# A 3x3 convolution by four products for two neighbouring columns, in a four-layer kernel on one Trainium2 core

## The chip, the cores and the metric

The kernel runs on one core of one Trainium2 chip. The metric is the device time of the whole program in microseconds (us). Before the change it is 9030.84 us, the median of three runs from 9029.97 to 9038.97 us. The engines are TensorE (PE, its weight loads PEld), VectorE (DVE), ScalarE (ACT), GpSimd (POOL) and SyncE (SP).

## What is computed

Four layers in a row on x of shape (16, 192, 32, 32), all in f32. The change touches layer 0 alone. Per image, `seq` is the image as 1024 positions of 192 channels:

```python
x1 = _vil_block(seq, ln_w, ln_b, w_up, ...)       # norm, up, causal filter, gated scan, norm, gate, down, + seq
x2 = silu(seq @ w_lin + b_lin)
y = x1 + x2                                       # (16, 192, 32, 32)
y = conv_general_dilated(y, conv2_w, (1, 1), ((1, 1), (1, 1)))     # 192 to 192 channels, 3 x 3
y = y + conv2_b
y = (y - mean) / sqrt(var + 1e-05) * bn_g + bn_b  # mean, var over images and positions
return where(y >= 0, y, 0.01 * y)
```

The kernel stores the convolution's result with its bias in the DRAM tensor `y`, with statistics for mean and variance; what follows is done when layer 1 reads it.

## The kernel before, in words

All engines run their own list of instructions; the order in each list is written out by hand in `stages`, and semaphores (`S.mark`, `wait_ge(*S(...))`) tie the lists together. Each part of the work is a generator with the same number of `yield` steps on every engine, so that a step stands at the same place in every list. For image b of layer 0:

- five steps of `conv(b - 1)`;
- eight steps of `project(b)`: ACT makes `xa` (line 844) from the filter that DVE ran in the join (lines 738 and 742); PE the gates (911) and then q and k (934), DVE and ACT the gates' arithmetic (794 to 886);
- two more steps of `conv(b - 1)`, and then the rest of `project`: PE's decay products (942, 948), DVE's `gam` (830) and `qt` (836);
- the scan, 24 steps (`chunks`), woven with the other 11 of `conv(b - 1)`; from its ninth step on also with `ahead(b + 1)`, the norms of the next image (lines 472 to 527 and 680 to 765). PE makes scores (1052), the outputs (1017, 1022), the state (1031) and transposes (1040, 1045); DVE spreads q (1086), multiplies (1099, 1105) and updates the state (1072, 1078); ACT takes exponentials (1131) and copies the outputs (1119); POOL adds the mask (966) to rows that SP fetches (979, 991);
- the norm of the scan's outputs (DVE 1150 to 1176, ACT 1186 to 1194), woven with `enter(b + 1)`, PE's up products (705, 708);
- the join: `lin` (1212 to 1218), transposes (1226), gates of the next image (898), `down` (1239, 1237), DVE's skip and gate (1255, 1257), and y in three parts (1264): y 0 is channels 0 to 127 of image rows 0 to 15, y 1 channels 128 to 191 of both halves of the rows (one half on partitions 0 to 63, the other on 64 to 127), y 2 channels 0 to 127 of rows 16 to 31.

The convolution reads the padded images `ypa` (34 x 34) and `ypb` (18 x 34 for each half; ACT copies the row of the other half, lines 1278 and 1279, 64x32). It has 18 steps, all f32. In the first nine, one for each tap, PE makes outputs 0 to 127 in two banks, one for each half of the rows: two products 128 to 128 on 512 columns (1298) and two 64 to 128 on the upper and the lower rows of the array (1300). In the other nine it makes outputs 128 to 191 of both halves in one bank: two products 128 to 64 (1312) and two 64 to 64 (1314). ACT evacuates with the bias to `yo` (1326), DVE takes bn_stats (1334), SP stores (1340, 1344).

PSUM is eight banks of 512 f32 columns, handed out in turn (`Banks.take`; `hold` keeps a bank out of the turn until `drop`): who is given a bank waits until the last user's data were read.

## Time and profile before

| | before |
|---|---|
| median of the runs | 9030.84 us |
| profiled execution, time | 9027.38 us |
| profiled execution, span | 9025.6 us, mean granted PE clock 0.899 |
| PE busy | 7558.3 us, 84% of the span |
| DVE busy | 5897.5 us, 65% |
| ACT busy | 3432.4 us, 38% |
| POOL busy | 1928.0 us, 21% |

Layer 0 takes the first fifteen of the profile's forty slices. One image's pass of its loop is some 206 us. In the profile a line number is that of the kernel; one f32 product of PE stands as two records.
### The profile page before, as it was taken

How to read it: one execution, taken by the hardware profiler on the slowest of the kernel's cores; microseconds unless marked ns; L12 is line 12 of the kernel's file. 1: busy time of each engine (PE TensorE's matmuls, PEld its weight loads, DVE VectorE, ACT ScalarE, POOL GpSimd, SP SyncE). 2: the span in 40 equal slices, each digit the busy share in tenths (PEclk: the TensorE clock that was granted, in tenths of full speed). 3: DMA queues.
4: the chain of work that ended last, by engine and by line, in shares of the span. 5: the costliest groups of instructions: out<-in, count | busy, mean ns of one | idle time of the engine just before them, and what ended most of it. 6: DMA issues, size and time to landing. Idle time of an engine off the chain costs nothing.

```text
span 9025.6 us, 92796 instructions
## 1 busy us (share of the span) xinstructions
PE 7558.3 (84%) x34478; PEld 3447.9 (38%) x34478; DVE 5897.5 (65%) x10339; ACT 3432.4 (38%) x6408; POOL 1928.0 (21%) x1639
## 2 busy tenths in 40 slices
PE   7999999999999994678888888888888888888855
PEld 4444444444444441133333333333333333333333
DVE  4666666666666654267766766776776776676645
ACT  3443343433434322443343254253344334334410
POOL 1111111111111110031331232142143133123223
PEclk8999999999999995779988989888898998888987
DMA  1111111111111111034544445454455454454446
GB/s 63 36 36 36 36 41 37 44 45 42 39 37 36 36 34 66 14 130 123 143 154 123 130 153 145 109 163 142 109 163 153 120 151 154 112 138 154 135 125 171
DMA packets 251362, 874.73 MB, mean 97 GB/s; under 512 B 47436, under 2 KB 50200, under 8 KB 250528
## 3 DMA queue, kind: packets, MB, share of 16 engines
q1 hardware_dynamic: 157440, 413.88, 17.1%
q0 software_dynamic: 92160, 453.06, 15.8%
q8 instruction: 274, 4.49, 0.2%
q10 hardware_dynamic: 1312, 1.87, 0.1%
q14 instruction: 176, 1.44, 0.1%
HBM read 614.69 MB, written 102.26 MB: 79 GB/s over the span
## 4 chain that ended last, share of the span: by engine, by line
PE 62%; DVE 18%; ACT 8%; DMA 4%; issue 3%; SPq 3%; POOL 0%; ACTq 0%; DVEq 0%; POOLq 0%
PE ps L2115 9%; PE ps L2348 6%; PE ps L2551 4%; PE ps L1052 4%; PE ps L1298 3%; DVE arena L1825 3%; PE ps L1022 3%; PE ps L2125 3%; SPq L2585 3%; PE ps L934 3%; PE ps L2562 3%; PE ps L2053 2%; DMA arena<-arena 2%; PE ps L2039 2%; PE ps L1300 2%
## 5 line engine op out<-in xcount | busy, mean ns | idle before, releaser
L2381 POOL DMA_INDIRECT arena<-img,arena x1152 | 1368.1, 1188 | 2845.4 <-DMA img<-arena 1988.8
L966 POOL TENSOR_TENSOR arena<-arena 128x512 f32<-128x512 f32 x384 | 438.0, 1146 | 2773.3 <-DMA arena<-decay 2773.3
L2242 DVE SCALAR_TENSOR_TENSOR arena<-arena 128x384 f32<-128x384 f32 x1152 | 745.7, 647 | 431.1 <-DMA arena<-img,arena 426.9
L1825 DVE TENSOR_REDUCE arena<-ps 128x2 f32<-128x1024 f32 x768 | 896.2, 1218 | 192.6 <-PE ps L2094 187.3
L1969 ACT ACTIVATE arena<-ps 128x512 f32<-128x512 f32 x1536 | 816.9, 603 | 395.7 <-PE ps L2125 394.5
L2551 PE MATMUL ps<-arena 128*64 128x512 f32 x3072 | 803.0, 651 | 137.0 <-DMA arena<-arena 136.9
L2115 PE MATMUL ps<-arena 128*64 128x512 f32 x3072 | 911.0, 697 | 0.0
L2348 PE MATMUL ps<-arena 128*96 128x128 f32 x4608 | 649.3, 304 | 110.5 <-DVE arena L2231 110.5
L2348 PEld LDWEIGHTS ps<-arena 128*96 128x96 f32 x4608 | 605.9, 186 | 265.4 <-issue 265.4
L2125 PE MATMUL ps<-arena 32*128 32x512 bf16 x1536 | 352.3, 433 | 227.2 <-ACT arena L1976 128.1
L1052 PE MATMUL ps<-arena 128*128 128x512 f32 x768 | 452.0, 673 | 81.8 <-DVE arena L1072 47.4
L934 PE MATMUL ps<-arena 128*128 128x512 f32 x1152 | 507.2, 596 | 0.0
L1099 DVE TENSOR_TENSOR arena<-ps,arena 128x512 f32<-128x512 f32 x384 | 265.7, 692 | 327.6 <-PE ps L1052 291.0
L2248 DVE SCALAR_TENSOR_TENSOR arena<-arena 128x192 f32<-128x192 f32 x1152 | 477.3, 415 | 0.0
L1131 ACT ACTIVATE arena<-arena 128x128 f32<-128x128 f32 x1536 | 476.4, 389 | 0.4
L2551 PEld LDWEIGHTS ps<-arena 128*64 128x64 f32 x3072 | 213.8, 145 | 542.8 <-issue 542.5
L1086 DVE COPY arena<-arena 32x128 f32<-32x128 f32 x1536 | 402.3, 262 | 16.8
L2094 PE MATMUL ps<-arena 32*128 32x512 bf16 x1536 | 293.7, 425 | 119.2 <-DVE arena L1825 93.8
L1022 PEld LDWEIGHTS ps<-arena 128*128 128x128 f32 x3072 | 390.5, 199 | 0.0
L1022 PE MATMUL ps<-arena 128*128 128x33 f32 x3072 | 390.5, 273 | 0.0
L2513 ACT ACTIVATE arena<-ps 128x512 f32<-128x512 f32 x128 | 76.7, 600 | 819.7 <-PE ps L2551 819.7
L2125 PEld LDWEIGHTS ps<-arena 32*128 32x128 bf16 x1536 | 75.7, 93 | 787.0 <-ACT arena L1969 577.0
(334 smaller groups left out, 11585.1 us busy)
## 6 DMA issues: line engine op xcount, KB each, us to landing
arena<-arena SPq DMA_DIRECT2D x1024, 144.5 KB, 2.8
arena<-decay SPq DMA_DIRECT2D x384, 256.0 KB, 3.3
img<-arena SPq DMA_DIRECT2D x162, 384.0 KB, 2.4
arena<-y SPq DMA_DIRECT2D x32, 768.0 KB, 5.7
arena<-img,arena POOLq DMA_INDIRECT x1152, 4.6
arena<-x SPq DMA_DIRECT2D x32, 384.0 KB, 6.5
y<-arena SPq DMA_DIRECT2D x32, 384.0 KB, 3.2
out<-arena SPq DMA_DIRECT2D x16, 768.0 KB
```

Source lines behind the costliest of these rows:

```text
L934: i = pe.matmul(ps[:, :], w[:, c, 128 * m:128 * m + 128], xa[:, c, H(h)], start=c == 0, stop=c == 2)
L1022: i = pe.matmul(po[:, 33 * h:33 * h + 33], px[:, 128 * j:128 * j + 128], v1[:, 33 * h:33 * h + 33], start=False, stop=j == 3)
L1052: pe.matmul(ps[:, :], kk[:, g, sl], self.qd[n % 3].rearrange("p a b -> p (a b)"), start=True, stop=True).then_inc(*S.mark("s_pe", b, n))
L1825: dve.tensor_reduce(out, self.wides[B.at("max", b, g, n, h) // 2].rearrange("p (a b) -> p a b", a=2), AX.X, AL.max).then_inc(*S.mark("max_ ...
L1969: act.activation(self.p[n % 6], B("score", b, n)[:, :], ACT.Exp).then_inc(*S.mark("p_act", b, n))
L2115: pe.matmul(o[64 * m:64 * m + 64, :], self.va[:, tb, 64 * hd:64 * hd + 64], self.p[n % 6], start=tb == 0, stop=tb == 7).then_inc(*S.mark(" ...
L2125: pe.matmul(ps[:, :], ks[r, hd // 3, 128 * tb:128 * tb + 128], qs[r, hd // 3, H(h)], start=True, stop=True).then_inc(*S.mark("score_pe", b ...
L2242: dve.scalar_tensor_tensor(gb[:, 0:384], gb[:, 384:768], pp[:, 1, n:n + 1], gb[:, 0:384], AL.mult, AL.add).then_inc(*S.mark("corner_x", b, n))
L2248: dve.scalar_tensor_tensor(self.tk[n // 9 % 2][:, n % 9, :], gb[:, 192:384], pp[:, 0, n:n + 1], gb[:, 0:192], AL.mult, AL.add).then_inc(*S ...
L2348: i = pe.matmul(ps[0:96, 128 * k:128 * k + 128], tk[:, tap, 96 * k:96 * k + 96], C["ID"], start=tap == 0, stop=tap == 8)
L2381: pool.indirect_dma_start(self.g[n % 6], None, img, bass.IndirectOffsetOnAxis(ap=ii[:, n:n + 1], axis=0)).then_inc(*S.landed(f"gather{n % ...
L2551: i = pe.matmul(ps[64 * t:64 * t + 64, :], self.dg[J % 2][:, o:o + 2, :].rearrange("p a b -> p (a b)"), win, start=n == 0, stop=n == 2)
```

## The change

For two neighbouring columns 2n and 2n + 1 of the output and each row y of the filter g, four products take the place of six. With d0 to d3 the four input columns 2n to 2n + 3 of the padded image, the input parts are d0 - d2, d1 + d2, d2 - d1 and d3 - d1, the filter parts g0, (g0 + g1 + g2)/2, (g0 - g1 + g2)/2 and g2. The product of part 1 and the one of part 2 with their sum and difference, and parts 0 and 3 on top of these, give the two columns.

- Filter parts: DVE makes them once in the setup, eight instructions on 576 elements, behind `prep0`. Part 1 takes the place of g1, part 2 is `u2`.
- Images: `ya` (34 x 34) and `yb`, now 50 x 34: rows 0 to 33 of it on partitions 64 to 127 and 16 to 49 on 0 to 63 are the whole padded image. ACT therefore copies 16 rows each way (64x512). Both lie where the scan's outputs `osb` and the gates `gb` lie, and POOL clears them in each norm.
- Input parts: POOL makes them in the join from every second column. "upper" (four instructions, 17 x 16) after y 0, "last" (four of 64 partitions, 34 x 16) after both halo copies, "lower" (four, 17 x 16) after y 2. `va` lies over `zs`, whose next writer waits for the convolution's end.
- Products: 18 steps in three thirds (outputs 0 to 127 of either half of the rows, outputs 128 to 191), each in two banks, two steps for each row of the filter. All have 256 columns. A step of the first two thirds is two products 128 to 128 and two 64 to 128; one of the last third four 128 to 64 and four 64 to 64, one for each quarter of the array.
- Evacuation: ACT takes one product with the bias (256 columns), DVE adds 512 columns, then 256 twice, then bn_stats, for each third; the y stores wait for DVE. Each stands at steps 7, 13 and 19 instead of 10 (two at once) and 19.

POOL no longer clears `ypa` and `ypb` in the setup, and the arena in SBUF grows by 700 columns. The diff, without context lines and without these two:

```diff
@@ -556,9 +556,13 @@
+        yr = Arena(ar.tile, ar.at)
-        self.ypa = ar([128, 34, 34])
-        self.ypb = ar([128, 18, 34])
+        self.ya, self.yb = yr([128, 34, 34]), yr([128, 50, 34])
+        self.va = [z.rearrange("p a b -> p (a b)")[:, 0:2176].rearrange("p (q r n) -> p q r n", q=4, r=34) for z in self.zs]
+        self.vb = ar([128, 2, 34, 16])
+        self.u2 = ar([128, 2, 3, 192])
+        self.p1 = ar([128, 256])
@@ -636,6 +640,16 @@
+        for k in range(2):
+            u = self.u2[:, k]
+            g = [W["C2"][:, k, :].rearrange("p (y x n) -> p y x n", y=3, x=3)[:, :, x, :] for x in range(3)]
+            dve.tensor_tensor(u, g[0], g[2], AL.add).then_inc(*S.mark("prep0", "u", k, 0))
+            dve.wait_ge(*S("prep0", "u", k, 0))
+            dve.tensor_tensor(u, u, g[1], AL.subtract).then_inc(*S.mark("prep0", "u", k, 1))
+            dve.wait_ge(*S("prep0", "u", k, 1))
+            dve.scalar_tensor_tensor(g[1], u, 0.5, g[1], AL.mult, AL.add).then_inc(*S.mark("prep0", "u", k, 2))
+            dve.wait_ge(*S("prep0", "u", k, 2))
+            dve.tensor_scalar(u, u, 0.5, None, AL.mult).then_inc(*S.mark("prep0", "u", k, 3))
@@ -768,6 +782,7 @@
+        act.wait_ge(*S("conv_pe", b - 2, 2))
@@ -848,6 +863,7 @@
+        act.wait_ge(*S("parts", b - 1, "lower"))
@@ -1255,17 +1271,15 @@
-        for n, inner in enumerate((self.ypa[:, 1:17, 1:33], self.ypb[:, 1:17, 1:33], self.ypa[:, 17:33, 1:33])):
+        for n, inner in enumerate((self.ya[:, 1:17, 1:33], self.yb[:, 17:33, 1:33], self.ya[:, 17:33, 1:33])):
-            dve.wait_ge(*S("conv_pe", b - 1, 2))
-            if n == 1:
-                dve.wait_ge(*S("halo", b - 1, 1))
+            dve.wait_ge(*S("zero", "pad", b))
@@ -1275,71 +1289,107 @@
-        act.activation(ypb[0:64, 17, 1:33], ypb[64:128, 1, 1:33], ACT.Copy).then_inc(*S.mark("halo", b, 0))
-        act.activation(ypb[64:128, 0, 1:33], ypb[0:64, 16, 1:33], ACT.Copy).then_inc(*S.mark("halo", b, 1))
+        act.activation(yb[0:64, 33:49, 1:33], yb[64:128, 17:33, 1:33], ACT.Copy).then_inc(*S.mark("halo", b, 0))
+        act.activation(yb[64:128, 1:17, 1:33], yb[0:64, 17:33, 1:33], ACT.Copy).then_inc(*S.mark("halo", b, 1))
+    def pool_norm(self, pool, b):
+        yield from skip(7)
+        pool.wait_ge(*self.S("norm_dve", b, "inv"))
+        pool.memset(self.ya, 0.0)
+        pool.memset(self.yb, 0.0).then_inc(*self.S.mark("zero", "pad", b))
+        yield
+    def pool_join(self, pool, b):
+        S, ya, yb, va, vb = self.S, self.ya, self.yb, self.va[b % 2], self.vb
+        parts = ((0, 2, AL.subtract), (1, 2, AL.add), (2, 1, AL.subtract), (3, 1, AL.subtract))
+        pool.wait_ge(*S("zero", "pad", b))
+        for key, r0, r1 in (("upper", 0, 17), ("last", 0, 34), ("lower", 17, 34)):
+            if key == "last":
+                pool.wait_ge(*S("conv_pe", b - 1, 2))
+                pool.wait_ge(*S("halo", b, 1))
+                for n, q in enumerate((0, 3, 1, 2)):
+                    h, (i, j, op) = n // 2, parts[q]
+                    if n == 2:
+                        pool.wait_ge(*S("parts", b, "upper"))
+                    r, y = slice(64 * h, 64 * h + 64), yb[64 * h:64 * h + 64, 16 - 16 * h:50 - 16 * h, :]
+                    t = pool.tensor_tensor(vb[r, n % 2], y[:, :, i:i + 31:2], y[:, :, j:j + 31:2], op)
+            else:
+                pool.wait_ge(*S("join_dve", b, "y", 0 if key == "upper" else 2))
+                if key == "lower":
+                    pool.wait_ge(*S("parts", b, "last"))
+                for q, (i, j, op) in enumerate(parts):
+                    t = pool.tensor_tensor(va[:, q, r0:r1, :], ya[:, r0:r1, i:i + 31:2], ya[:, r0:r1, j:j + 31:2], op)
+            t.then_inc(*S.mark("parts", b, key))
+    def filter_part(self, k, y, q, m):
+        return self.u2[:, k, y, m] if q == 2 else self.W["C2"][:, k, 576 * y + 192 * (q, q, 0, 2)[q]:576 * y + 192 * (q, q, 0, 2)[q] + 192][:, m]
-        S, B, W = self.S, self.B, self.W["C2"]
+        S, B, va, vb, part = self.S, self.B, self.va[b % 2], self.vb, self.filter_part
-        out = []
-        for h in range(2):
-            ps, free = B.hold(("conv", b, h), ("conv_act", b, h))
-            pe.wait_ge(*free)
-            out.append(ps)
-        pe.wait_ge(*S("join_dve", b, "y", 2))
-        pe.wait_ge(*S("halo", b, 1))
-        for tap in range(9):
-            y, x = divmod(tap, 3)
-            w = slice(192 * tap, 192 * tap + 128)
-            for h in range(2):
-                pe.matmul(out[h][:, :], W[:, 0, w], self.ypa[:, 16 * h + y:16 * h + y + 16, x:x + 32], start=tap == 0, stop=False)
-            for h, r in enumerate(both):
-                i = pe.matmul(out[h][:, :], W[r, 1, w], self.ypb[r, y:y + 16, x:x + 32], start=False, stop=tap == 8)
-                if tap == 8:
-                    i.then_inc(*S.mark("conv_pe", b, h))
-            yield
-        for h in range(2):
-            B.drop(("conv", b, h))
-        ps, free = B.hold(("conv", b, 2), ("conv_act", b, 2))
-        pe.wait_ge(*free)
-        for tap in range(9):
-            y, x = divmod(tap, 3)
-            w = slice(192 * tap + 128, 192 * tap + 192)
-            for h, r in enumerate(both):
-                pe.matmul(ps[r, :], W[:, 0, w], self.ypa[:, 16 * h + y:16 * h + y + 16, x:x + 32], start=tap == 0, stop=False)
-            for h, r in enumerate(both):
-                i = pe.matmul(ps[r, :], W[r, 1, w], self.ypb[r, y:y + 16, x:x + 32], start=False, stop=tap == 8)
-            if tap == 8:
-                i.then_inc(*S.mark("conv_pe", b, 2))
-            yield
-        B.drop(("conv", b, 2))
+        flat = lambda v: v.rearrange("p r n -> p (r n)")
+        pe.wait_ge(*S("prep0", "u", 1, 3))
+        pe.wait_ge(*S("parts", b, "lower"))
+        for n in range(3):
+            banks = []
+            for q, by in enumerate(("first", "y")):
+                ps, free = B.hold(("conv", b, n, q), ("conv_dve", b, n, by))
+                pe.wait_ge(*free)
+                banks.append(ps)
+            out = [banks[q in (1, 2)][:, 256 * (q in (2, 3)):256 * (q in (2, 3)) + 256] for q in range(4)]
+            m = slice(128, 192) if n == 2 else slice(0, 128)
+            halves = list(enumerate(both)) if n == 2 else [(n, slice(0, 128))]
+            for y in range(3):
+                for n2, pair in enumerate(((0, 1), (3, 2))):
+                    rows = lambda h: slice(16 * h + y, 16 * h + y + 16)
+                    for q in pair:
+                        for h, r in halves:
+                            pe.matmul(out[q][r, :], part(0, y, q, m), flat(va[:, q, rows(h), :]), start=y == 0 and n2 == 0, stop=False)
+                    for t, q in zip(both, pair):
+                        for h, r in halves:
+                            i = pe.matmul(out[q][r, :], part(1, y, q, m)[t], flat(vb[t, n2, rows(h), :]), start=False, stop=y == 2 and n2 == 1)
+                    if y == 2 and n2:
+                        i.then_inc(*S.mark("conv_pe", b, n))
+                    yield
+            for q in range(2):
+                B.drop(("conv", b, n, q))
+        S = self.S
+        for n in range(3):
+            yield from skip(6)
+            act.wait_ge(*S("conv_pe", b, n))
+            act.wait_ge(*S("conv_dve", b if n else b - 1, n - 1 if n else 2))
+            act.activation(self.p1, self.B("conv", b, n, 1)[:, 0:256], ACT.Identity, bias=self.W["C2B"][:, n // 2:n // 2 + 1]).then_inc(*S.mark("conv_act", b, n))
+    def dve_conv(self, dve, b):
-            if n != 1:
-                yield from skip(9)
-            act.wait_ge(*S("conv_pe", b, n))
-            act.activation(self.yo[:, n, :], B("conv", b, n)[:, :], ACT.Identity, bias=self.W["C2B"][:, n // 2:n // 2 + 1]).then_inc(*S.mark("conv_act", b, n))
-    def dve_conv(self, dve, b):
-        S = self.S
-        for n in range(3):
-            if n != 1:
-                yield from skip(9)
+            yield from skip(6)
+            one, two = B("conv", b, n, 0), B("conv", b, n, 1)
+            y = self.yo[:, n, :].rearrange("p (n s) -> p s n", s=2)
+            dve.tensor_tensor(y, one.rearrange("p (s n) -> p s n", s=2), self.p1.unsqueeze(1).to_broadcast([128, 2, 256]), AL.add).then_inc(*S.mark("conv_dve", b, n, "first"))
+            dve.wait_ge(*S("conv_dve", b, n, "first"))
+            dve.tensor_tensor(y[:, 0, :], y[:, 0, :], two[:, 256:512], AL.add)
+            dve.tensor_tensor(y[:, 1, :], y[:, 1, :], two[:, 256:512], AL.subtract).then_inc(*S.mark("conv_dve", b, n, "y"))
+            dve.wait_ge(*S("conv_dve", b, n, "y"))
-        yield from skip(9)
-        sp.wait_ge(*S("conv_act", b, 1))
+        yield from skip(12)
+        sp.wait_ge(*S("conv_dve", b, 1, "y"))
-        yield from skip(9)
-        sp.wait_ge(*S("conv_act", b, 2))
+        yield from skip(6)
+        sp.wait_ge(*S("conv_dve", b, 2, "y"))
@@ -1389,7 +1439,7 @@
-                    lambda b: skip(8), lambda b: None, lambda b: skip(18))
+                    lambda b: self.pool_norm(e, b), lambda b: self.pool_join(e, b), lambda b: skip(18))
...
```

## Rows read from the trace of the kernel before

**Rows 1.** the page, second part: TensorE's busy tenths in forty slices of the span

```profile
PE   7999999999999994678888888888888888888855
```

**Rows 2.** timeline of PE, join to gates: start us, us, engine line operation

```profile
669.06 2.85 PE L1226 MATMUL ps<-arena 128*128 128x128 f32 x24 [1.15 <-DVE arena L1176]
...
686.08 1.98 PE L1298 MATMUL ps<-arena 128*128 128x512 f32 x4 [1.14 <-DVE arena L1264]
687.99 1.13 PE L1300 MATMUL ps<-arena 64*128 64x512 f32 x4
689.05 1.99 PE L1298 MATMUL ps<-arena 128*128 128x512 f32 x4
...
700.95 2.79 PE L911 MATMUL ps<-arena 128*64 128x512 f32 x12
```

**Rows 3.** timeline of PE, products of 256 columns: layer 3, then layer 2

```profile
7040.02 7.17 PE L2532 MATMUL ps<-arena 96*128 96x256 f32 x32 [0.31 <-DVE arena L2441]
...
4234.32 7.99 PE L2307 MATMUL ps<-arena 96*32 96x256 f32 x144 [1.25 <-ACT arena L2274]
```

**Rows 4.** timeline of PE, products to the next norm

```profile
737.11 1.88 PE L1298 MATMUL ps<-arena 128*128 128x512 f32 x4
...
742.96 0.24 PE L942 MATMUL ps<-arena 76*128 76x8 bf16 x3
...
748.54 2.04 PE L1052 MATMUL ps<-arena 128*128 128x512 f32 x2 [1.93 <-DVE arena L1086]
...
767.90 1.08 PE L1312 MATMUL ps<-arena 128*64 128x512 f32 x4
...
769.92 1.13 PE L1052 MATMUL ps<-arena 128*128 128x512 f32 x2
...
838.60 1.81 PE L1052 MATMUL ps<-arena 128*128 128x512 f32 x2 [3.34 <-DVE arena L1072]
...
875.12 2.85 PE L1226 MATMUL ps<-arena 128*128 128x128 f32 x24 [1.15 <-DVE arena L1176]
```

**Rows 5.** timeline of VectorE, join, y 1 and y 2

```profile
682.22 0.69 DVE L1264 TENSOR_TENSOR arena<-ps,arena 128x512 f32<-128x512 f32 x1 [0.25 <-PE ps L1237]
...
685.34 0.69 DVE L1264 TENSOR_TENSOR arena<-ps,arena 128x512 f32<-128x512 f32 x1
```

**Rows 6.** ScalarE: durations min/median/max of line 755, then two rows of its timeline

```profile
L755 ACT ACTIVATE arena<-arena x32: 621/626/630, 62.2 to 3090.3; 64x512 f32<-64x512 f32 x32
...
690.74 1.06 ACT L844 ACTIVATE arena<-arena 128x1024 f32<-128x1024 f32 x1 [4.22 <-DVE arena L742]
...
737.93 1.05 ACT L886 ACTIVATE arena<-arena 12x1024 bf16<-12x1024 f32 x1
```

**Rows 7.** GpSimd by line, durations ns min/median/max

```profile
L966 POOL TENSOR_TENSOR arena<-arena x384: 1087/1093/2077, 121.1 to 3294.7; 128x512 f32<-128x512 f32 x192
...
L2571 POOL TENSOR_TENSOR arena<-arena x64: 1498/1508/1527, 4075.8 to 8976.7; 128x768 f32<-128x768 f32 x64
```

**Rows 8.** VectorE by line, durations ns min/median/max, with and without GpSimd at work

```profile
L824 DVE TENSOR_TENSOR arena<-arena x16: 1521/1903/2141, 122.5 to 3200.7; 12x1024 f32<-12x1024 f32 x16
...
L827 DVE TENSOR_TENSOR arena<-arena x16: 1211/1214/1216, 129.6 to 3207.8; 12x1024 f32<-12x1024 f32 x16
```

**Rows 9.** windows (PE clock last but two), then timeline of PE

```profile
842.00:844.00 2.00, 2.00 (x6) 0.56 (x6) 0.41 (x2) 1.56 (x5) 0.00 (x0) 0.50 0.00 0
3328.00:3330.00 2.00, 2.00 (x10) 1.70 (x8) 1.97 (x4) 0.00 (x0) 0.00 (x0) 0.50 0.00 0
...
3324.72 5.38 PE L1226 MATMUL ps<-arena 128*128 128x128 f32 x24 [14.54 <-DVE arena L1176]
```

**Rows 10.** timeline of VectorE, opening of the scan, and behind the scan

```profile
743.54 3.68 DVE L836 TENSOR_TENSOR arena<-arena,ps 128x512 f32<-128x512 f32 x6
...
852.37 0.69 DVE L1334 BATCH_NORM_STATS2 arena<-arena 128x6 f32<-128x512 f32 x1 [2.57 <-ACT arena L1326]
```

**Rows 11.** waits of VectorE from 669.06 to 875.12: us in total, times, longest

```profile
DVE arena L1099 <- PE ps L1052: 20.5, 12, 4.7
```

12 lines of the change are left out of this document (6 added, 6 removed).

## The prediction

> **What bounds the kernel now.** I read first the page's slices: in the first fifteen of the forty, which are layer 0, TensorE's (PE's) digit is 9 but for the first [rows 1]. Then the order of time on PE in one batch of layer 0, from the transposes at 669.06 us to the same transposes of the next batch at 875.12 us [rows 2, 4]: 206.1 us a batch. In it PE's starts follow each other with hardly a gap. So layer 0 is bound by PE's program order, but closely followed by VectorE (DVE): where PE does wait, DVE releases it, before line 1052 at 748.54 us (1.93 us) and at 838.60 us (3.34 us) and before 1226 (1.15 us) [rows 4]. The convolution of batch b lies in four places: five steps right after the join, two after the q and k products, eleven woven into the scan of batch b+1; for the last batch all eighteen in a row. What a step saves is worth what that place allows, so I work place by place and take the batch from 669 to 875 us as the model of fifteen.
>
> **The product itself.** An old step with 128 outputs is 1.91 us for the two full products and 1.06 us for the pair on half the rows, 2.97 together (starts at 686.08, 687.99 and 689.05) [rows 2]. An old step of the last 64 outputs is 2.02 us, from 767.90 to 769.92 [rows 4]. One f32 product stands as two records. 256 columns cost 0.22 us a record (32 in 7.17 us), and with four column tiles at work 0.055 us (144 in 7.99 us) [rows 3]. So of the old step 4 x 0.44 + 2 x 0.44 = 2.64 us is streaming and 0.33 us is what the two switches between full and half rows cost; in the 64-output step 1.76 is streaming and 0.26 switches. A new step keeps both switches and halves the columns: 4 x 0.22 + 2 x 0.22 + 0.33 = 1.65 us. For the 64 outputs: two pairs of column tiles, 0.88 us, then eight records in four quarters at 0.055 us, 0.44 us, and 0.26: 1.58 us. The quarters are not in the trace of before; four column tiles are the nearest row. If they ran two by two, the step would be 2.02 us; I take 1.58. In all 9 x 2.97 + 9 x 2.02 = 44.9 us become 12 x 1.65 + 6 x 1.58 = 29.3 us: 15.6 us less PE work a batch, 250 us over sixteen. That is what would be gained if PE's order alone set the time.
>
> **Place A, the join and the first five steps.** Before, PE starts them when the last third of y is written (DVE line 1264, starts 685.34), at 686.08, and reaches line 911 at 700.95: 14.87 us [rows 2, 5]. Now the parts by GpSimd (POOL) come between. The part "last" needs y 1 (start 682.22, 0.69 us) and both halo copies on ScalarE (ACT), now 64x512 instead of 64x32, 0.63 us each [rows 5, 6]: it can begin at 684.2 at the earliest. It is four POOL subtractions or sums of 544 elements. POOL needs 1.09 us for 512 and 1.51 us for 768 [rows 7]: by the line through both 544 cost 1.14 us, by proportion 1.16; 4.6 us. Then "lower", queued behind it on POOL, four of 272: 0.70 us by the line, 0.58 by proportion, 2.3 to 2.8 us. Without contention PE would start at 691.1 to 691.6, 5.0 to 5.5 us late. But now POOL works while DVE runs its filter (line 742). DVE's line 824, which always meets POOL's masks, takes 1.90 us in the median (1.52 to 2.14), and line 827, of the same shape, 1.21 us without them [rows 8]. So "upper" (2.8 us of POOL from y 0 on) puts about 1 us on the DVE work ahead of y 1, and POOL itself is held up in turn; no row shows by how much (its maximum for 512 is 2.08 us, its median 1.09 [rows 7]), I take a fifth. That makes the start 8 us late, with 5.0 and 10 as ends.
>
> The Trainium skill (GPSIMD Engine Reference, Key points) says that GpSimd shares its SBUF interfaces with VectorE, with contention against instructions with two SBUF inputs. The trace agrees: 1.90 against 1.21 us.
>
> PE idles through all of this, about 9 us. After a long idle stretch its clock is low: in the last batch PE starts after 14.5 us of idling at 3324.72, the granted clock is 0.50 (1.2 GHz) until 3330, and line 1226 takes 5.38 us where it takes 2.85 in the other batches [rows 9, 4]. After the 3.34 us gap at 838.60 the clock is 0.50 and still so at 844 [rows 4, 9]. A restart thus loses 2.5 to 3.3 us; I take 2.8. Before, the five steps ran without it. Five steps save 14.87 - 8.25 = 6.6 us. A = 8 - 6.6 + 2.8 = +4.2 us, ends +0.9 (5.0 late, 2.5 for the clock) and +6.7 (10 late, 3.3). xa, which line 911 needs, is no new limit: its third ACT instruction starts at 690.74 [rows 6], and even 4 us later it is ahead of line 911. The q and k stage behind it is unchanged and moves as a whole.
>
> **Place C, two steps and the evacuation of the first third.** Before: 737.11 to 742.96, then the decay products, and DVE's line 836 from 743.54, which opens the scan [rows 4, 10]. Now PE would be through at 740.4 (2 x 1.65). But in DVE's order the sums of third 0 now stand ahead of the qt products: ACT ends line 886 at 739.0 [rows 6], then evacuates 256 columns, some 0.5 us (512 take 0.63 [rows 6]), DVE adds 512 (0.61, a sixth of line 836's 3.68 [rows 10]), twice 256 (0.4, between half and all of 0.61), bn_stats 0.6, and about 0.3 us for the new semaphores: 741.8, the copy of gam, and line 836 at 742.0. C = -1.6 us; ends -2.5 (PE alone decides) and 0.
>
> **Place D, eleven steps in the scan.** Before two of 2.97 and nine of 2.02; now five of 1.65 and six of 1.58. The savings are 2 x 1.32 + 3 x 0.37 + 6 x 0.44 = 6.4 us. DVE follows too closely to give it all: in the whole batch it waits only 20.5 us, twelve times, for the scores of line 1052 [rows 11], and the sums of third 1, 2.1 us with semaphores less 0.6 for the bn_stats that was here before, fall near 790 us, where DVE is occupied. The last third needs two banks again, and the ring gives it just those of third 1, so PE stands until DVE has made its sums; queued behind that are the next scores. Before, the last third held one bank. I take 2 us for both: D = -4.4 us, ends -6.4 and -1.5.
>
> **Place E, scan to norm.** The chain from the last o copy to line 1226 is DVE and ACT: bn_stats of the last third at 852.37 stands right ahead of the norm's sums, and PE waits at 875.12 [rows 4, 10]. Two more waits and adds of 0.61 and 2 x 0.4 stand there now, ACT is 0.2 us shorter: E = +1.4 us, ends +0.7 and +2.0. Clearing ya and yb on POOL lies beside DVE work that waits for ACT anyway: nothing; its cover gone, at most 6.1 us (2856 elements at POOL's 1.09 us for 512 of two inputs [rows 7]), and only if DVE had to wait for all of it. The y store on SP waits for DVE at the same slot of the order as DVE's own sums, with the next decay rows queued behind it; those wait for the same DVE product, so nothing.
>
> **The sum.** 4.2 - 1.6 - 4.4 + 1.4 = -0.4 us a batch, fifteen times: -6. Once: eight DVE instructions of 576 elements on the setup's chain, 0.7 to 0.8 us each, +6; the last batch, 8 + 2.8 + 1.5 - 15.6 = -3. Together -3 us on the profiled execution's 9027.38 us (span 9025.6). The median of the runs is 3.5 us above it, so 9030.84 - 3 = about 9028. The 250 us of products saved are given back as waiting.
>
> **Rivals.** Faster: POOL is undisturbed, start 5.3 us late, and DVE takes the scan's savings in its idle time. A +1.5, C -2.0, D -5.4, E +1.2: -4.7 a batch, about 8960 us; with C and D at their ends about 8935. For it: DVE does have 20.5 us of waits [rows 11]. Against: they lie at other places than the new sums.
> Slower: POOL is what the join waits for, place A. Past a start 8.4 us late the batch loses. At 11 us late, with D at -3, it is 7.2 - 1.6 - 3.0 + 1.4 = +4.0 a batch, about 9095 us. For it: the 2.08 us maximum [rows 7], and that POOL now meets DVE all through the join. Its reads take every second f32, which no row has. The Trainium skill (GPSIMD Engine Reference, Performance pitfalls for Q7 kernels) gives half as much again per element for reads with steps above 8 bytes; here the step is exactly 8, so by the page this stays out; no row here shows either.
> Not what it says: the quarters run two by two, +0.44 x 6 = +2.6 us a batch and some of it hidden, about 9060 us.
>
> **Chances.** About 0.2%, 18 us or 1.2 us a batch, is what a measurement can tell from no change. Near balance (2.5 us a batch either way) 0.35, of which 0.25 within 18 us and 0.05 beyond on each side; the faster rival 0.30; the slower 0.28; the quarters 0.07, of it 0.02 within. Faster 0.35, same 0.27, slower 0.38. Both signs hold most of it; the balance case's own range is 8990 to 9068. The range for 8 in 10 takes in most of both rivals and leaves 1 in 10 below 8940 and 1 in 10 above 9110.
>
> **What the profile would show.** New steps 1.65 and 1.58 us apart at full clock, in the quarters eight records in about 0.44 us; PE idle about 9 us before the first new step, released by POOL, clock 0.50 behind it; DVE's line 836 about 1.6 us earlier against the q and k products; a wait of PE for DVE at the last third's banks; the norm's first sum 1.4 us later after the scan. Wrong if PE's wait for POOL is under 6 us or over 11, or if the scan shortens by more than 6 us or not at all.

## The result and the profile after

The changed kernel takes 9202.3 us (median of four runs, 9187.0 to 9207.3) against 9030.4 us for the kernel before beside it: ratio 1.0192, 95% interval 1.0169 to 1.0216. It is 172 us slower, where 9028 us and a range of 8940 to 9110 us were predicted. The profiled execution has a span of 9201.7 us against 9025.6, and a mean granted TensorE clock of 0.872 against 0.899.

The page of the kernel after, busy us, share and instructions of each engine, PE's busy tenths and its granted clock in forty slices, then the group of the new full products:

```profile
PE 7497.4 (81%) x35246; PEld 3602.2 (39%) x35246; DVE 6034.5 (66%) x10491; ACT 3437.6 (37%) x6408; POOL 2226.3 (24%) x1861
...
PE   7888888888888885668888888888878888888865
...
PEclk8988888998898896679898889988888888898877
...
L1354 PE MATMUL ps<-arena 128*64 128x256 f32 (+1 forms) x1536 | 385.2, 467 | 213.5 <-POOL arena L1322 173.1
```

PE is busy only 61 us less, where the products removed were priced at 250. Its digits in the slices of layer 0 are 8 where they were 9 [rows 1]. The loss lies there: the last batch's transposes start at 3496.0 instead of 3324.7 us [rows 9] (+171.3), that batch's convolution gives 7 us back, and layers 1 to 3, whose code is the same, read some 12 us longer (0.2%; not followed up).

One batch again, transposes at 694.20 to transposes at 912.55 us (218.4 us; before 206.1 [rows 2, 4]). Timeline of PE in the kernel after: start us, us, engine line operation, and in brackets the idle time before it with what ended it. Line 1354 holds the full products (1298 and 1312 before), 1357 the half-row ones (1300, 1314), 927 the gates (911), 1068 the scores (1052), 1056 and 1061 the transposes (1040, 1045):

```profile
721.19 2.07 PE L1354 MATMUL ps<-arena 128*128 128x256 f32 x4 [11.11 <-POOL arena L1322]
723.19 1.23 PE L1357 MATMUL ps<-arena 64*128 64x256 f32 x4
...
729.20 1.13 PE L1354 MATMUL ps<-arena 128*128 128x256 f32 x4
730.26 0.70 PE L1357 MATMUL ps<-arena 64*128 64x256 f32 x4
730.90 1.13 PE L1354 MATMUL ps<-arena 128*128 128x256 f32 x4
731.96 0.70 PE L1357 MATMUL ps<-arena 64*128 64x256 f32 x4
732.59 2.80 PE L927 MATMUL ps<-arena 128*64 128x512 f32 x12
...
817.27 1.98 PE L1354 MATMUL ps<-arena 128*64 128x256 f32 x8 [2.88 <-DVE arena L1382]
819.18 1.13 PE L1357 MATMUL ps<-arena 64*64 64x256 f32 x8
820.24 2.07 PE L1068 MATMUL ps<-arena 128*128 128x512 f32 x2
...
851.04 0.55 PE L1056 MATMUL ps<-arena 128*128 128x128 f32 x3 [1.32 <-DVE arena L1088]
...
853.41 1.68 PE L1068 MATMUL ps<-arena 128*128 128x512 f32 x2 [1.49 <-DVE arena L733]
...
860.88 2.07 PE L1068 MATMUL ps<-arena 128*128 128x512 f32 x2
...
872.20 1.13 PE L1068 MATMUL ps<-arena 128*128 128x512 f32 x2
...
877.79 0.90 PE L1061 MATMUL ps<-arena 128*128 128x128 f32 x3 [3.07 <-DVE arena L1088]
```

Three things are to be seen. The first step starts 27.0 us behind the transposes (before 17.0), after 11.1 us of waiting for POOL. At full clock the steps are 1.70 us apart (729.20, 730.90). And behind the gap of 2.88 us, behind the two of 1.32 and 1.49 us together, and behind the one of 3.07 us, a pair of scores takes 1.92 to 2.07 us where it takes 1.13 at 872.20: the clock is half. Behind the first of the two small gaps alone it was not; the transposes at 851.04 still ran at full speed.

GpSimd in the same join, line 1322 the parts "upper" and "lower", line 1316 "last", and then the same in the last batch, where VectorE has no filter to run:

```profile
705.21 4.85 POOL L1322 TENSOR_TENSOR arena<-arena 128x272 f32<-128x272 f32 x4 [20.73 <-DVE arena L1278]
710.02 7.71 POOL L1316 TENSOR_TENSOR arena<-arena 64x544 f32<-64x544 f32 x4
717.88 3.26 POOL L1322 TENSOR_TENSOR arena<-arena 128x272 f32<-128x272 f32 x4
...
3507.63 2.45 POOL L1322 TENSOR_TENSOR arena<-arena 128x272 f32<-128x272 f32 x4 [18.72 <-DVE arena L1278]
3511.68 4.39 POOL L1316 TENSOR_TENSOR arena<-arena 64x544 f32<-64x544 f32 x4 [1.59 <-ACT arena L1293]
```

The same 544 elements cost 1.10 us undisturbed and 1.93 beside the filter.

Windows of the batch in each kernel, in three stretches: transposes to first score, and the scan in two parts. Columns: stretch, us, busy time of PE, PEld, DVE, ACT, POOL, then the granted PE clock, DMA share and GB/s. The kernel before:

```profile
669.06:748.54 79.48, 72.68 (x231) 29.77 (x232) 42.96 (x61) 24.28 (x37) 5.21 (x4) 0.99 0.04 14
748.54:800.00 51.46, 51.45 (x272) 31.51 (x272) 39.12 (x119) 21.18 (x66) 13.14 (x12) 0.95 0.32 93
800.00:851.00 51.00, 46.10 (x222) 25.90 (x220) 30.28 (x79) 18.77 (x52) 9.71 (x9) 0.93 0.11 37
```

The kernel after, and six microseconds of it around the wait that ends at 817.27 and six behind the one that ends at 853.41:

```profile
694.20:778.40 84.20, 67.30 (x232) 31.65 (x232) 48.55 (x65) 25.19 (x36) 21.83 (x17) 0.90 0.05 13
778.40:830.00 51.60, 48.47 (x274) 34.31 (x275) 42.37 (x120) 20.76 (x66) 13.19 (x12) 0.90 0.30 92
830.00:888.50 58.50, 51.67 (x269) 31.55 (x267) 29.88 (x80) 18.98 (x52) 8.81 (x8) 0.82 0.10 32
...
817.00:823.00 6.00, 5.73 (x23) 2.89 (x24) 4.02 (x11) 0.00 (x0) 1.09 (x1) 0.50 0.39 131
855.00:861.00 6.00, 6.00 (x16) 2.99 (x14) 1.16 (x2) 1.33 (x4) 0.87 (x1) 0.50 0.15 48
```

Length times (1 - clock) is an estimate of what the clock costs in a stretch; it is too high where PE would otherwise have waited. In the scan: before 51.46 x 0.05 + 51.00 x 0.07 = 6.1 us, after 51.6 x 0.10 + 58.5 x 0.18 = 15.7 us. The scan is 102.5 us before and 110.1 after. Less this estimate it is 96.4 and 94.4: by it the change made the scan 2 us shorter, and the clock takes 9.6 us more than before. PE's idle time in the scan, length less busy time, is 4.9 us before and 10.0 after.

That the clock lengthens the scan can be seen within one execution of the kernel after, whose fourteen scans run the same instructions. PE's idle time in them is 9.4 to 11.0 us. The three shortest take 106.7 to 106.8 us and lose 12.1 to 12.2 us by the estimate, the two longest take 113.7 us and lose 20.6 to 20.7. There a microsecond of loss is worth 0.8 us of time.

Waits of PE from 450 to 3300 us (us in total, times, longest), the kernel before:

```profile
PE ps L1052 <- DVE arena L1072: 41.8, 13, 3.3
PE ps L1052 <- DVE arena L1086: 26.6, 14, 1.9
```

The kernel after (line 1088 is the state's copy, 1072 before; 1382 the sums of a third; 733 the norm's centring):

```profile
PE ps L1354 <- POOL arena L1322: 144.4, 13, 11.1
PE ps L1061 <- DVE arena L1088: 40.0, 13, 3.1
PE ps L1354 <- DVE arena L1382: 35.5, 13, 3.0
PE ps L1068 <- DVE arena L1102: 20.7, 13, 1.9
PE ps L1068 <- DVE arena L733: 19.4, 13, 1.5
...
PE ps L1056 <- DVE arena L1088: 17.2, 13, 1.3
```

Before, one wait of more than 1.2 us stands in the second half of the scan, 3.3 us. After, there are four: 2.9, 1.3, 1.5 and 3.1 us.

### The profile page after: what moved, and what is told of

Same layout as the page of the kernel before. It is cut to its first block, busy times and chain, and to the rows that moved or that the text cites. A ratio compares the mean times of both kernels' runs of the same rounds, so it can differ in the third digit from the quotient of the medians.

```text
span 9201.7 us, 94787 instructions
## 1 busy us (share of the span) xinstructions
PE 7497.4 (81%) x35246; PEld 3602.2 (39%) x35246; DVE 6034.5 (66%) x10491; ACT 3437.6 (37%) x6408; POOL 2226.3 (24%) x1861
## 3 DMA queue, kind: packets, MB, share of 16 engines
q10 hardware_dynamic: 1312, 1.87, 0.1%
## 4 chain that ended last, share of the span: by engine, by line
PE 59%; DVE 19%; ACT 9%; issue 4%; DMA 4%; SPq 3%; POOL 3%; ACTq 0%; DVEq 0%; POOLq 0%
PE ps L2165 9%; PE ps L2398 6%; PE ps L2601 4%; PE ps L1068 4%; PE ps L1354 3%; PE ps L1038 3%; DVE arena L1875 3%; PE ps L2175 3%; SPq L2635 3%; PE ps L950 3%; PE ps L2612 3%; PE ps L2103 2%; DMA arena<-arena 2%; PE ps L1357 2%; PE ps L2089 2%
## 5 line engine op out<-in xcount | busy, mean ns | idle before, releaser
L1875 DVE TENSOR_REDUCE arena<-ps 128x2 f32<-128x1024 f32 x768 | 896.7, 1218 | 191.0 <-PE ps L2144 185.6
L2019 ACT ACTIVATE arena<-ps 128x512 f32<-128x512 f32 x1536 | 817.2, 603 | 402.3 <-PE ps L2175 401.2
L1354 PE MATMUL ps<-arena 128*64 128x256 f32 (+1 forms) x1536 | 385.2, 467 | 213.5 <-POOL arena L1322 173.1
L1068 PE MATMUL ps<-arena 128*128 128x512 f32 x768 | 486.4, 720 | 57.9 <-DVE arena L1102 31.1
L950 PE MATMUL ps<-arena 128*128 128x512 f32 x1152 | 507.2, 597 | 0.0
L1038 PEld LDWEIGHTS ps<-arena 128*128 128x128 f32 x3072 | 410.9, 208 | 0.0
L2621 POOL TENSOR_TENSOR arena<-arena 128x768 f32<-128x768 f32 x64 | 95.9, 1510 | 1208.3 <-PE ps L2601 1208.0
```

Source lines behind the costliest of these rows:

```text
L950: i = pe.matmul(ps[:, :], w[:, c, 128 * m:128 * m + 128], xa[:, c, H(h)], start=c == 0, stop=c == 2)
L1038: i = pe.matmul(po[:, 33 * h:33 * h + 33], px[:, 128 * j:128 * j + 128], v1[:, 33 * h:33 * h + 33], start=False, stop=j == 3)
L1068: pe.matmul(ps[:, :], kk[:, g, sl], self.qd[n % 3].rearrange("p a b -> p (a b)"), start=True, stop=True).then_inc(*S.mark("s_pe", b, n))
L1354: pe.matmul(out[q][r, :], part(0, y, q, m), flat(va[:, q, rows(h), :]), start=y == 0 and n2 == 0, stop=False)
L1875: dve.tensor_reduce(out, self.wides[B.at("max", b, g, n, h) // 2].rearrange("p (a b) -> p a b", a=2), AX.X, AL.max).then_inc(*S.mark("max_ ...
L2019: act.activation(self.p[n % 6], B("score", b, n)[:, :], ACT.Exp).then_inc(*S.mark("p_act", b, n))
```

## The experiments

The runs were made on several chips. The kernel before takes about 9170 us on three of them and 9029 on the fourth; each ratio is against it on the same chip. The difference lies behind layer 0: from the last batch's transposes to the end the kernel before takes 5701 us, and before_two_banks, which has the same code there, 5840 us. Up to the first score the two read the same in the table, so stages of layer 0 are compared directly. Four kernels (before_two_banks, before_half, fill, one_bank) were run once, so their totals have no interval. The table gives means of the first fourteen batches, in us behind the batch's transposes: first convolution step, first decay product (line 942 before, 958 after), first score, first up product (the scan's end), next transposes. "Clock" is the time lost to it between the decay products and the up products, length x (1 - granted clock), mean of twelve batches; "rest" is that stretch's length less this loss. Both are estimates, and single batches spread around the means: the scans of the kernel after take 106.7 to 113.7 us.

| kernel | step | decay | score | up | next | clock | rest |
|---|---|---|---|---|---|---|---|
| before | 17.0 | 73.9 | 79.5 | 181.9 | 206.0 | 6.2 | 101.8 |
| after | 27.0 | 77.7 | 84.0 | 193.6 | 217.8 | 16.5 | 99.4 |
| no_parts | 17.0 | 65.0 | 71.3 | 180.8 | 205.8 | 16.4 | 99.4 |
| no_sums | 27.0 | 77.7 | 83.3 | 194.7 | 218.8 | 17.6 | 99.4 |
| hold_first | 27.0 | 77.7 | 84.0 | 194.5 | 218.8 | 16.6 | 100.2 |
| filter_late | 22.4 | 72.4 | 78.7 | 189.7 | 214.0 | 17.3 | 100.0 |
| project_first | 61.5 | 73.3 | 79.4 | 190.4 | 214.7 | 18.0 | 99.1 |
| before_two_banks | 17.0 | 73.9 | 79.5 | 190.8 | 214.9 | 14.0 | 102.9 |
| before_half | 17.0 | 73.9 | 79.5 | 177.8 | 202.1 | 7.7 | 96.2 |
| fill | 27.0 | 77.0 | 83.3 | 193.2 | 217.4 | 8.6 | 107.6 |
| one_bank | 27.0 | 77.1 | 83.4 | 196.2 | 222.6 | 20.6 | 98.5 |
| weave22 | 27.0 | 77.0 | 83.3 | 191.0 | 215.4 | 15.8 | 98.2 |
| before_weave22 | 17.0 | 73.9 | 79.5 | 191.1 | 216.0 | 14.7 | 102.5 |
| filter_weave22 | 22.4 | 72.6 | 78.9 | 184.6 | 208.9 | 13.1 | 98.9 |
| filter_weave16 | 22.4 | 72.7 | 79.0 | 183.2 | 208.0 | 12.2 | 98.6 |
| filter16_warm | 22.4 | 71.3 | 77.6 | 185.2 | 210.4 | 15.9 | 98.0 |

### The parts left out

```diff
-        for key, r0, r1 in (("upper", 0, 17), ("last", 0, 34), ("lower", 17, 34)):
+        for key, r0, r1 in ():
...
-        pe.wait_ge(*S("parts", b, "lower"))
+        pe.wait_ge(*S("join_dve", b, "y", 2))
+        pe.wait_ge(*S("halo", b, 1))
```

> The changed kernel without GpSimd's input parts: va and vb hold old values, so this leaves out the twelve subtractions and sums and with them PE's wait for them; PE starts the convolution once y 2 and the halo copies are there. Theory 1 (the join and the scan lose separately: the join by the wait for GpSimd and the low clock behind it, the scan by banks and VectorE's sums): the join goes from +6.5 us against the kernel before to -6.4, the scan stays at +7.6; 16 x 12.9 = 206 us less than the changed kernel's 9202, about 8996 us. Rival (the scan's loss is a consequence of the disturbed join, through the clock or the phase in which it starts): the scan comes back too, 4 us a batch faster than before, about 8830 us.

Measured: ratio 0.9969 (0.9949 to 0.9990). The join is as before (17.0), and the five steps save 6.4 us (gates at 25.5 instead of 31.9); to the decay products the batch is 8.9 us ahead of the kernel before. By the next transposes 0.2 us of it is left; besides, only the last batch gains, whose eighteen steps stand in a row. The scan is 109.5 us, as in the kernel after. So the scan's loss does not come from the late start. Against the kernel before the batch is 8.9 us ahead at the decay products and 8.2 at the first score, and the scan takes 7.1 us more; another 0.9 goes between the scan and the next transposes.

### The sums left out

```diff
-            dve.tensor_tensor(y, one..., self.p1..., AL.add).then_inc(*S.mark("conv_dve", b, n, "first"))
-            dve.tensor_tensor(y[:, 0, :], y[:, 0, :], two[:, 256:512], AL.add)
-            dve.tensor_tensor(y[:, 1, :], y[:, 1, :], two[:, 256:512], AL.subtract).then_inc(*S.mark("conv_dve", b, n, "y"))
-                ps, free = B.hold(("conv", b, n, q), ("conv_dve", b, n, by))
+                ps, free = B.hold(("conv", b, n, q), ("conv_act", b, n))
```

> The changed kernel without VectorE's three additions for each third: the output is missing its sums; ScalarE's 256 columns alone free both banks. Theory 1 (handover of third 1's banks to the last third behind VectorE's sums, 2.9 us of PE wait a batch, with the clock drop it starts, plus 1.5 us of sums at the scan's opening): the scan goes from +7.6 to about 0, the opening 1.3 us earlier, about 9 us a batch, 9065 us. Rival (what the scan lost is the ring being one bank shorter while the next image's norms run, which stays): only 2.9 + 1.3 us a batch, about 9140 us.

Measured: ratio 1.0188 (1.0160 to 1.0216), scan 111.4 us. Taking DVE's new work away, and with it the wait for it at the banks, gains nothing; PE waits at other places instead (22.1 us in all at line 1068 for the state's copy, a wait that the kernel after does not have in its list). The 2 us that the prediction put on the sums and the handover are not what the scan loses.

### Both banks of the second third given back early

```diff
+            if n == 2:
+                for q in range(2):
+                    B.drop(("conv", b, 1, q))
             ...
-            for q in range(2):
-                B.drop(("conv", b, n, q))
+            if n != 1:
+                for q in range(2):
+                    B.drop(("conv", b, n, q))
```

The second third's banks stay out of the turn until the last third has taken two others.

> The changed kernel, but the last third takes its two banks before third 1's are dropped, so that it gets other ones; nothing is left out. Theory 1 (the handover wait of 2.9 us and the clock drop from it, 6 us at half clock): -4 us a batch, about 9140 us, with PE's wait before the first step of the last third gone. Rival (VectorE is behind by its sums anyway, and PE meets it at the next score): the same 9200 us, the wait being at line 1068 instead.

Measured: ratio 1.0198 (1.0163 to 1.0234). The wait of 2.9 us at line 1354 is gone, and one of 4.1 us at line 1056 stands in its place; the scan takes 110.5 us. Waits of PE in this kernel:

```profile
PE ps L1056 <- DVE arena L1088: 67.2, 26, 4.1
PE ps L1061 <- DVE arena L1088: 40.0, 13, 3.1
```

### The filter behind the parts

```diff
-            run(some(self.filter, 4 if n == 2 else 2))
+            if n == 2:
+                dve.wait_ge(*S("parts", b, "lower"))
+                run(some(self.filter, 8))
```

> The changed kernel, but VectorE runs none of the filter's eight join instructions until GpSimd's parts are done; nothing is left out. Theory 1 (GpSimd is slowed by these two-input instructions: 544 elements cost 1.93 us beside them, 1.10 in the last batch, where there is no filter): upper 2.5, last 4.4 and lower 2.5 us of GpSimd, PE starts 22.2 us after the transposes instead of 27.0, -4.8 us a batch, about 9130 us. Rival (the filter, 9.3 us after the parts, then keeps line 927 waiting): PE idles there instead, and the gain is under 1.5 us a batch, about 9185 us.

Measured: ratio 1.0123 (1.0090 to 1.0156). GpSimd alone, the timeline of POOL (lines shifted by two):

```profile
706.45 2.45 POOL L1324 TENSOR_TENSOR arena<-arena 128x272 f32<-128x272 f32 x4 [20.73 <-DVE arena L1278]
710.76 4.41 POOL L1318 TENSOR_TENSOR arena<-arena 64x544 f32<-64x544 f32 x4 [1.86 <-ACT arena L1295]
715.31 2.46 POOL L1324 TENSOR_TENSOR arena<-arena 128x272 f32<-128x272 f32 x4
```

The start comes 5.4 us behind that of the kernel before, as the prediction's sum without contention had it (5.0 to 5.5). The other 4.6 us of the ten are thus the contention with the filter: "last" takes 4.41 us instead of 7.71, "lower" 2.46 instead of 3.26, and "last" starts 0.5 us earlier. The scan stays long (111.0).

### The next projection ahead of the convolution's first steps

```diff
-            run(some(g, 5))
             p = project(b)
             run(some(p, 8))
-            run(some(g, 2))
+            run(some(g, 7))
```

> The changed kernel with the first five steps of the convolution moved behind the eight steps of gates, q and k, next to the two that stand there; nothing is left out. Theory (the join loses 10 us of waiting for GpSimd and 3 us of low clock; gates and q and k, which need only xa, can take that place): line 927 starts about 26 us after the transposes, when xa is there, instead of 38.3; five steps of 1.69 us come back behind; -4 us a batch, about 60 us less than the changed kernel. Rival (xa, whose filter GpSimd slows, comes so late that PE idles and loses its clock all the same): line 927 at 30 us or later, no gain or a loss.

Measured: ratio 1.0161 (1.0139 to 1.0182). PE no longer waits for POOL, but for `xa`:

```profile
PE ps L927 <- ACT arena L859: 108.0, 42, 6.6
```

The decay products come 4.4 us earlier than after the change; 1.3 us of this is lost in the scan.

### A second held bank, in the kernel before

```diff
+        pe.wait_ge(*B.hold(("conv", b, 3), ("conv_act", b, 2))[1])
...
+        B.drop(("conv", b, 3))
```

Nothing else is changed: the last third takes a bank that it does not use.

> The kernel before; its last nine steps hold a second bank that nothing is written to. Nothing is left out. Theory 1 (the scan's loss is the ring, one bank shorter while the next image's norms run): waits of PE for VectorE's state update and mean appear as in the changed kernel, the scan goes from 102.4 us a batch to 107 to 111, the granted clock is low for 25 us or more of it instead of 12, and the whole is 1.0 to 1.5% slower. Rival (PE has less to do in the scan, and its clock falls for that): the scan stays within 1 us of 102.4, the whole within 0.2%.

Measured, one run: 9298.4 us against 9170.6 (1.014). The scan grows from 102.4 to 111.3 us. Waits of PE in it:

```profile
PE ps L1045 <- DVE arena L1072: 40.0, 13, 3.1
PE ps L1052 <- DVE arena L1086: 21.2, 13, 1.7
PE ps L1052 <- DVE arena L719: 19.4, 13, 1.5
```

and the windows of the batch, as above:

```profile
770.96:822.00 51.04, 50.40 (x263) 30.78 (x263) 39.43 (x115) 21.44 (x67) 13.16 (x12) 0.96 0.30 93
822.00:882.46 60.46, 53.95 (x232) 30.08 (x231) 30.45 (x83) 18.99 (x52) 9.70 (x9) 0.83 0.10 31
```

The waits of 1.5 and 3.1 us that the kernel after has, and the low clock behind them, appear here with the old products. A bank less in turn shifts who waits for whom. This is what was expected, the scan just past the upper end (107 to 111 us). Of the 8.9 us a batch, 7.8 are clock (6.2 to 14.0 in the table) and about 1 is the rest.

### Half the columns in the last third, in the kernel before

```diff
-                pe.matmul(ps[r, :], W[:, 0, w], self.ypa[:, 16 * h + y:16 * h + y + 16, x:x + 32], ...)
+                pe.matmul(ps[r, 0:256], W[:, 0, w], self.ypa[:, 16 * h + y:16 * h + y + 8, x:x + 32], ...)
```

(The half-row products likewise; half of the outputs 128 to 191 is left out.)

> The kernel before, but the nine steps of outputs 128 to 191 run on 256 of their 512 columns: half of this third of the result is left out. Banks, VectorE and ScalarE as before. Theory 2 (less PE work in the scan makes its clock fall, and that takes the saving back): 7.9 us less work a batch at full clock, but the scan is shorter by less than 2 us and the low-clock time goes from 12 to 20 us and more. Rival (the ring did it): the scan is 6 to 8 us shorter, 95 us, and the whole 1.1 to 1.4% faster than before.

Measured, one run: 9092.3 us (0.991). Products removed with nothing added gain 4.1 us in the scan (3.9 a batch) of the 5.6 that "rest" shows; the clock's cost grows by 1.5. This lies between the two expectations: neither is most of the saving lost, nor all of it kept.

### The last third's products made twice, in the kernel after

```diff
+                    for rep in range(2 if n == 2 else 1):
```

(around the two loops over `q`; `start` and `stop` only at the ends, so that the last third's sums are doubled.)

> The changed kernel, but each step of the last third runs its products twice (so that its sums are doubled): 9.6 us more PE work a batch at full clock. Theory 2 (the clock falls in the scan for want of PE work): the low-clock time in the scan goes from 33 us to under 20, and the scan, 109.5 us, becomes at most 2 us longer or even shorter. Rival (PE's work sets the scan's time, waits as they are): 118 to 120 us and the low clock as it is.

Measured, one run: 9328.5 us (1.017), against 1.019 of the kernel after in its own comparison. "Rest" grows by 8.2 us, and the clock's cost falls by 7.9, from 16.5 to 8.6. Some 9.6 us more of products a batch (six steps of 1.6) cost 0.3 us of scan, as the theory of the clock expected. The change met the converse: products taken out of this stretch brought nothing.

### One bank for the last third, in the kernel after

```diff
-            for q, by in enumerate(("first", "y")):
+            for q, by in enumerate(("first", "y") if n < 2 else ("y",)):
...
-                    for q in pair:
+                    for rep, q in enumerate(pair if n < 2 else pair[:1] * 2):
```

(As many full products as before, half as many half-row ones, on two quarters of the array instead of four, all into one bank. A step takes PE 1.08 and 0.65 us as before; the last third's sums are not those of the convolution.)

> The changed kernel, its last third in one bank instead of two: parts 1 and 2 of outputs 128 to 191 are left out, and parts 0 and 3 run their full-row products twice, so that a step of the last third takes PE as long as before (1.6 us). VectorE's and ScalarE's instructions stand as they were. Theory 1 (the second bank is what costs the scan its 7 us): the scan goes from 109.5 us a batch to 100 to 103, the low clock in it from 33 us to 12 to 18. Rival (something else of the change, such as shorter steps between the scores): 108 us or more.

Measured, one run: 9377.7 us (1.023): scan 112.8 us, clock 20.6. The bank that alone lengthened the kernel before does not, given back, shorten the kernel after. PE still waits for the sums ahead of the last third, 1.8 us here, and 3.6 us for the state's copy at a score. The theory that the second bank is the whole cause falls here.

### The steps earlier in the scan

One line in `stages`, in the kernel after, in it with the filter behind the parts, and in the kernel before:

```diff
-            weave((scan(b), 24), (g, 11))
+            weave((scan(b), 24), (g, 22))
```

> The changed kernel with the eleven steps of the convolution woven into the first half of the scan (22 to the scan's 24 instead of 11), so that no bank is held for it when the next image's norms run; nothing is left out. Theory 1 (the ring one bank short beside the norms costs the scan 7 us): the waits for the mean's bank and for the state's update shrink, the low clock in the scan goes from 33 us to under 20, the scan from 109.5 to about 102 us, the whole 110 us less than the changed kernel. Rival (with no products left between the scores PE meets VectorE at every one of them in the second half): the scan stays at 107 us or more.

> filter_late and weave22 together; nothing is left out. If the two act apart: 214.0 us a batch in filter_late less what weave22 gives, 7 us, so 207 us, about the kernel before (206.0), ratio 1.00 to 1.01. If the later scan's VectorE is the limit, 1.01 to 1.02 as filter_late.

> The kernel before with the convolution's eleven steps woven into the first half of the scan; nothing is left out. Here five banks are in turn instead of four in the changed kernel. Theory 1: little to win, as its ring of five is nearly enough: the scan, 102.4 us, changes by under 3 us. Rival (products between the scores matter more than banks): the scan becomes 5 us longer.

Measured: weave22 1.0169 (1.0152 to 1.0186), filter_weave22 1.0048 (1.0031 to 1.0065), before_weave22 1.0175 (1.0158 to 1.0192). The same move gains 2.4 us a batch in the kernel after (7 were expected), 5.1 on top of the late filter, and costs the kernel before 10.0 (under 3 were expected, and 5 by the rival). In the last two it is mainly the clock column that moves (-4.2 and +8.5). In weave22 one execution holds scans of 104.4 us with 9.8 us lost by the estimate and scans of 112.1 with 23.9: half of that loss is paid. PE's idle time is 8.6 us in the former and 3.6 in the latter, so part of what the slow clock takes is time that PE would have waited. With 16 in place of 22 and the late filter:

> filter_late with the eleven steps woven in the first two thirds of the scan (16 to 24); nothing is left out. Theory 1: between filter_late and filter_weave22 if the banks alone count: 209 to 212 us a batch. If products between the scores are needed as well, it is the best of the three, under 207 us.

Measured: 1.0052 (1.0030 to 1.0075), 208.0 us a batch, 2 us more than before. This and filter_weave22 are the best of the complete kernels with the new products, and both are still behind the kernel before. Here too neither expectation, 209 to 212 us or under 207, was met.

### PE kept busy while it waits for POOL

filter_weave16, with twelve records of products of 512 columns, whose result is not used, ahead of PE's wait:

```diff
+                for _ in range(6):
+                    pe.matmul(banks[0][:, :], self.C["ONE"], self.W["C2"][:, 0, 0:512], start=True, stop=True)
+                pe.wait_ge(*S("parts", b, "lower"))
```

> filter_weave16 with six products of constants on PE while it waits for GpSimd's parts (0.88 us each); nothing is left out. Theory (the low clock behind that wait costs 2.3 us a batch): the five steps take 8.5 instead of 10.8 us, the batch 205.7 instead of 208.0 us, the ratio to the kernel before 1.00 instead of 1.005. Rival (line 927 then waits for xa, which is late in this order): under 1 us a batch.

Measured: 1.0052 (1.0034 to 1.0071), no better. The timeline of PE shows that it did what it was made for:

```profile
705.23 5.31 PE L1349 MATMUL ps<-arena 128*128 128x512 f32 x12
711.90 1.13 PE L1359 MATMUL ps<-arena 128*128 128x256 f32 x4 [1.35 <-POOL arena L1324]
712.96 0.70 PE L1362 MATMUL ps<-arena 64*128 64x256 f32 x4
713.59 1.13 PE L1359 MATMUL ps<-arena 128*128 128x256 f32 x4
```

The first step runs at full clock, and the gates come at 30.9 instead of 33.2 us. But the clock's cost in the scan rises from 12.2 to 15.9 us, and the batch is longer (210.4 against 208.0). What was saved at one restart was lost again in the scan of this profile; why is not shown.

## Why the prediction was wrong

Working by its own steps, on the batches of the table; the sum was -0.4 us a batch and the batch measures +11.8. The forecast of 9028 us is 174 us too low.

- **The product.** Right. 1.70 us (729.20 to 730.90) against 1.65 predicted, and 1.61 against 1.58 for the last third. The last batch, all steps in a row at full clock (timeline of PE, kernel after):

```profile
3541.07 1.08 PE L1354 MATMUL ps<-arena 128*64 128x256 f32 x8
3542.08 0.66 PE L1357 MATMUL ps<-arena 64*64 64x256 f32 x8
3542.68 1.08 PE L1354 MATMUL ps<-arena 128*64 128x256 f32 x8
```

  Eight records in the four quarters take 0.60 us with their switch, so the quarters run together. The rival "two by two" is out.
- **Place A.** The mechanism right, a term mis-sized. Predicted +4.2 (ends +0.9 and +6.7), measured +6.5 (gates at 38.3 instead of 31.9). The start is 10.0 us late where I took 8: contention was priced at a fifth on POOL's time and measures three quarters (1.93 against 1.10 us). The clock's loss behind the wait is as predicted: five steps in 11.4 us instead of 8.5, 2.9 against 2.8. PE's wait is 11.1 us, not 9, just past what I had called wrong.
- **Place C.** Right. The two steps save 2.6 us (38.3 to 77.7 is 39.4, before 42.0), 0.7 of it is lost again until the first score: -1.9, predicted -1.6.
- **Place D.** This is the step that failed: predicted -4.4 (ends -6.4 and -1.5), measured +7.1 (109.5 against 102.4). That is 11.5 of the 12.2 us by which the batch misses the sum, and fifteen times 11.5 us is 172 us. The prediction had named a scan that does not shorten at all as a sign of being wrong. I had priced the saved products at the full-clock step and subtracted waits of a known length. Two terms failed. The sums and the handover were put at 2 us, and PE's idle time in this scan grew by 5.1 (4.9 to 10.0): 2.9 us at the banks, and then 1.3, 1.5 and 3.1 us where 3.3 stood. The larger term was put at nothing: what stands behind the waits, the low clock, although the rows showed it in this very scan: 0.50 at 842 to 844, behind a gap of 3.34 us [rows 4, 9]. I priced it in place A and not in place D. By the estimate it takes 15.7 us of the scan of this batch against 6.1; this and the idle time overlap in part, and the saved products stand against them. Up to the eleventh of the 24 scores all is as predicted (the batch is 0.3 us behind, from 4.7 at the first); then come 3.9 us at the bank handover and 9.6 between the scores 18 and 21, and 1.5 us are gained, net, between and behind them.
- **Place E.** +1.4 predicted, 0 measured (24.2 against 24.1): the norm's first sum does come 1.2 us later behind the scan (3.2 instead of 2.0), as predicted, but in the kernel before DVE then stands 2.02 us for ACT ahead of line 1166, and this wait is gone after the change. The sums took its place.
- **Once.** The setup's eight instructions cost 5.5 us, as predicted (6), but 4 of it is gone by the first transposes. The last batch gains 7 us instead of 3: no filter stands beside POOL there, and its start is late by the undisturbed sum.

The rival "slower", POOL at 11 us, had its sign and half its mechanism right: with the start 10 us late place A alone would give 9028 + 15 x 2.3 = 9063 us, inside the range. The rest is the scan.

What is shown: the scan's loss is there without the late join (no_parts) and without VectorE's sums (no_sums), and it is not undone by moving the one wait at the banks (hold_first, where 4.1 us of waiting took its place). It goes with the granted clock: in the windows, in the table, where "rest" is between 98.0 and 100.2 in all kernels that make the new products once, and within single executions. How much of the lost clock is paid in time differs (0.8 of it in the kernel after, half in weave22), so that "nearly all" of the loss is clock by the estimate, not by a separate measurement. One more held bank is able to bring it about (before_two_banks, +8.9 us of which 7.8 clock), and is not all of it (one_bank). Besides, the waits themselves grew by 5 us. What stays open is which of the small waits tips the clock, and why one order of the same work loses 12 us to it and another 18; in these runs moving any of them moved the others.

## What to carry to other kernels

Where TensorE is the bound and stands at full clock only because it hardly stops, price every wait that a change adds at its length plus the half-speed stretch behind it, in every place and not just at the longest wait; here waits of 1.3 to 3.1 us, 8.8 us in all, went with 15.7 us of lost clock in the scan. Products taken out of such a stretch, where VectorE follows closely behind, may bring nothing: look at length, granted clock and waits of the stretch together before counting instructions. And give work to GpSimd only after looking at what VectorE does in the same microseconds.

## What the runs showed of the hardware that I had not expected

- The same products of TensorE can cost nothing: with 9.6 us more of them a batch the scan is 109.9 us instead of 109.5 (fill, one run), and the clock's cost falls by 7.9 us.
- GpSimd's subtraction of 64 x 544 f32 elements takes 1.10 us alone and up to 2.12 us beside VectorE's filter (median 2.04 in the join); VectorE's scalar_tensor_tensor of 128 x 1024 takes 1.285 us alone and up to 2.03. Both engines pay; before the change the filter did not meet GpSimd and took 1276 to 1287 ns each time. Two instructions side by side take 2.0 us, less than the 2.4 of one after the other.
- GpSimd reading every second f32 cost nothing extra: 0.61 us for 272 and 1.10 us for 544 elements (a quarter of the four), below the line through the contiguous rows [rows 7], 0.70 and 1.14.
- Holding one PSUM bank more, unused, through the last nine of the eleven convolution steps in the scan costs the kernel before 1.4% (one run).
- Within one execution the same scan takes 106.7 to 113.7 us, with 12.1 to 20.7 us of lost clock, at nearly the same idle time of PE.
